# First attention of a vision tower on one core: whole-tile transfers of the operand parts, gathered by the reads, and projections by three products of split operands

## What is computed

```python
h = _L0_tok_ref(x, ...)                      # token mixer (attention-free), layer norm
h = concatenate([cls_tok, h], axis=1)        # one class token in front: 257 tokens
h = h + _L0_attn_ref(_layernorm(h), Wq, Wkv, Wout)
h = h + _L0_ffn_ref(_layernorm(h), ...)      # latent attention, then 8 experts, top 2

def _L0_attn_ref(tokens, Wq, Wkv, Wout):     # the "first attention"
    q = split_heads(tokens @ Wq, HEADS)      # 16 heads of 16
    kv = split_heads(tokens @ Wkv, HEADS)
    k, v = (kv[..., :DK], kv[..., DK:])      # 16 and 64 wide
    q, k, v = (l2norm(q), l2norm(k), l2norm(v))
    sim = jnp.einsum('bhid,bhjd->bhij', q, k)
    attn = jnp.square(jax.nn.relu(sim))
    out = tanh_norm(jnp.einsum('bhij,bhjd->bhid', attn, v))
    return merge_heads(out) @ Wout
```

## Time and profile before

| | |
|---|---|
| median of three runs | 3128.6 us (3127.97 to 3133.56) |
| the profiled execution | 3139.85 us, of which the profiled span is 3138.1 us |
| constants | 0 to about 52 us of the span |
| mixer and first attention, 32 samples | about 52 to 1630 us |
| PE busy over the span | 2907.1 us, 93% |
| DVE, ACT, POOL busy | 67%, 46%, 37% |

### The profile page before, as it was taken

One profiled execution on the slowest core, in us unless ns is written; L12 is line 12 of the kernel. 1 busy time (PEld: TensorE's weight loads), 2 busy tenths in 40 slices (PEclk: granted clock), 3 DMA queues, 4 the chain that ended last, 5 costly groups with the idle time before them and its releaser, 6 DMA issues. The chain is left out here.

```text
span 3138.1 us, 66657 instructions
## 1 busy us (share of the span) xinstructions
PE 2907.1 (93%) x21548; PEld 2217.3 (71%) x21549; DVE 2098.8 (67%) x5372; ACT 1442.7 (46%) x2948; POOL 1157.0 (37%) x966
## 2 busy tenths in 40 slices
PE   3899999999999999999966999999999972999998
PEld 1677777777777777777744666666766652999997
DVE  4577677677677777777734777777777855444444
ACT  0444544545545545445422555555555533444443
POOL 3324434434434334334321233333233324444443
PEclk7899999999999999999987999999999985999999
DMA  3424424424424424324302111111111101554544
GB/s 83 96 70 92 107 66 95 107 62 98 102 62 104 98 66 104 94 70 104 87 22 51 49 47 53 43 42 52 45 54 47 44 33 44 77 76 76 77 77 69
DMA packets 161126, 223.12 MB, mean 71 GB/s; under 512 B 30305, under 2 KB 125730, under 8 KB 161074
## 3 DMA queue, kind: packets, MB, share of 16 engines
q1 hardware_dynamic: 135138, 187.50, 23.9%
q0 software_dynamic: 25936, 34.95, 7.2%
HBM read 125.26 MB, written 97.08 MB: 71 GB/s over the span
## 5 line engine op out<-in xcount | busy, mean ns | idle before, releaser
L66 POOL TENSOR_TENSOR vrn<-vsm,inv_root 128x16 f32<-128x16 f32 x64 | 243.8, 3809 | 285.8 <-DVE vsm L836 285.8
L665 ACT ACTIVATE R<-psA 128x1024 f32<-128x1024 f32 x256 | 262.4, 1025 | 168.4 <-PE psA L1150 164.2
L857 DVE TENSOR_TENSOR PR<-R 128x1024 f32<-128x1024 f32 x256 | 321.3, 1255 | 0.0
L2512 POOL DMA_INDIRECT out_rows<-e_y,e_dest x137 | 213.7, 1560 | 289.8 <-DMA out_rows<-e_y,e_dest 182.2
L1904 DVE TENSOR_REDUCE m_nm<-psC 128x4 f32<-128x1028 f32 (+1 forms) x256 | 239.0, 956 | 72.0 <-PE psC L2177 71.4
L1165 PE MATMUL psA<-PR,V 128*64 128x258 f32 x2048 | 283.4, 398 | 0.0
L670 ACT ACTIVATE oTs<-psA 128x258 f32<-128x258 f32 x256 | 99.1, 387 | 358.1 <-PE psA L1165 352.3
L1783 ACT ACTIVATE m_PT<-psC 128x770 f32<-128x770 f32 x256 | 194.0, 810 | 137.3 <-PE psC L2205 137.3
L1210 PE MATMUL psA<-wout,OT 128*128 128x256 f32 x1024 | 244.6, 382 | 0.4 <-DVE OT L899 0.4
L1698 POOL DMA_INDIRECT xg<-tn,idx x124 | 124.5, 1004 | 318.6 <-DMA xg<-tn,idx 186.6
L1210 PEld LDWEIGHTS psA<-wout,OT 128*128 128x128 f32 x1024 | 188.7, 191 | 24.6 <-DVE OT L899 0.7
(11 more groups left out here) (417 smaller groups left out, 7633.0 us busy)
## 6 DMA issues: line engine op xcount, KB each, us to landing
ks<-kparts SPq DMA_DIRECT2D x256, 128.0 KB, 3.3
qs<-qparts SPq DMA_DIRECT2D x256, 128.0 KB, 3.8
e_x<-xg SPq DMA_DIRECT2D x143, 129.0 KB
xraw<-in_x SPq DMA_DIRECT2D x66, 256.0 KB
qparts<-qh SPq DMA_DIRECT2D x128, 128.0 KB, 2.4
kparts<-kh SPq DMA_DIRECT2D x64, 128.0 KB, 2.5
kparts<-kl SPq DMA_DIRECT2D x64, 128.0 KB, 2.4
qparts<-ql SPq DMA_DIRECT2D x64, 128.0 KB, 2.4
```

Source lines behind the costliest of these rows:

```text
L66: return pool.tensor_tensor(out, x, e.to_broadcast(list(out.shape)), ALU.pow)
L665: act.activation(R[:, p % 2].rearrange("p a t n -> p t a n"), ps[:, 0:2, :].rearrange("p t (a n) -> p t a n", a=2), ACT.Relu).then_inc(rel ...
L857: dve.tensor_tensor(PR[:, p % 2, :, :, 0:L], R[:, p % 2], R[:, p % 2], ALU.mult).then_inc(prob_done, 1)
L2512: pool.indirect_dma_start(out, bass.IndirectOffsetOnAxis(ap=dest[:, b % XD:b % XD + 1], axis=0), y[:, b % XD], None, compute_op=ALU.add).t ...
```

## The change

Five edits are made.

1. Each part goes to DRAM in one transfer of 128 partitions with 2 KB each (`keep_part`), so five stores instead of ten. `kh` is stored at `k_sq` and `qh` (twice) at `q_sq`, not after the lows. The DRAM tensors `kparts` and `qparts` have the head half `hh` as their first index, then the part n, so that one part lies in DRAM in two blocks of 64 rows.
2. The loads collect, for each of 32 partitions, four pieces of 1 KB instead of one of 4 KB (`heads`).
3. `project` uses split weights `wqkh`, `wqkl` and split tokens `xh`, `xl`, three fp32r products for each fp32 one. It waits for `xl_done` where it waited for `xT_done`; `token_lows` is moved ahead of `result` and `keep_sums` on DVE.
4. The constants stage splits `wqk`: DVE makes `wqk_hi` and `wqk_lo` ahead of the sums of squares, ACT lays both out by head (8 more small copies at its end).
5. `psq` shares the memory of `prl`; `class_products` waits for `xT_done` itself.

```diff
-            def keep_parts(tiles, rows, out):
-                for n, part in enumerate(tiles):
-                    for hh in range(2):
-                        sp.dma_start(rows[:, hh, n].rearrange("c x n -> x c n"),
-                                     part[64 * hh:64 * hh + 64].bitcast(F32)).then_inc(out, 16)
+            def keep_part(part, rows, n, out):
+                sp.dma_start(rows[:, n], part[:].bitcast(F32).rearrange("p c n -> p (c n)")).then_inc(out, 16)
+
+            def heads(rows, hh, n, c):
+                return rows[hh, n:n + 2].rearrange("a (r m) (c n) -> c (a r) m n", m=4, c=KT)[c]
...
-                        sp.dma_start(ks[to:to + 32, 4 * c:4 * c + 4].bitcast(F32).rearrange("p m n -> p (m n)"),
-                                     v.kparts[c, hh].rearrange("a (r m) n -> (a r) (m n)", m=4)).then_inc(moved, 16)
+                        sp.dma_start(ks[to:to + 32, 4 * c:4 * c + 4].bitcast(F32),
+                                     heads(v.kparts, hh, 0, c)).then_inc(moved, 16)
...
                 if c == 0:
+                    sp.wait_ge(k_sq, j + 1)
+                    keep_part(kh, v.kparts, 0, k_out)
                     sp.wait_ge(kl_done, j + 1)
-                    keep_parts((kh, kl), v.kparts, k_out)
+                    keep_part(kl, v.kparts, 1, k_out)
+                    sp.wait_ge(q_sq, j + 1)
+                    keep_part(qh, v.qparts, 0, q_out)
+                    keep_part(qh, v.qparts, 2, q_out)
                     sp.wait_ge(ql_done, j + 1)
-                    keep_parts((qh, ql, qh), v.qparts, q_out)
-                    sp.wait_ge(k_out, 64 * j + 64)
+                    keep_part(ql, v.qparts, 1, q_out)
+                    sp.wait_ge(k_out, 32 * j + 32)
                     lay_out_keys(0, moved0)
-                    sp.wait_ge(q_out, 96 * j + 96)
+                    sp.wait_ge(q_out, 48 * j + 48)
                     lay_out_queries(0, moved0)
...
                 prob(i, d, 5)
+                if more:
+                    token_lows(j)
                 if before:
                     result(i - 1)
                 keep_sums(i, d, 0)
                 if more:
-                    token_lows(j)
                     key_lows(j)
                     query_lows(j)
...
             def project(bank, first, done):
                 for c in range(2):
+                    sums = ps[:, bank, c * L:(c + 1) * L]
+                    cols = slice(first + c * P, first + (c + 1) * P)
                     for k in range(KT):
-                        last = pe.matmul(ps[:, bank, c * L:(c + 1) * L], v.wqk[:, k, first + c * P:first + (c + 1) * P],
-                                         xT[:, k, :], start=k == 0, stop=k == KT - 1)
+                        pe.matmul(sums, v.wqkh[:, k, cols], xh[:, k, :], start=k == 0, stop=False)
+                        pe.matmul(sums, v.wqkl[:, k, cols], xh[:, k, :], start=False, stop=False)
+                        last = pe.matmul(sums, v.wqkh[:, k, cols], xl[:, k, :], start=False, stop=k == KT - 1)
                 last.then_inc(done, 1)

             def project_keys(j):
-                pe.wait_ge(xT_done, j + 1)
+                pe.wait_ge(xl_done, j + 1)
                 project(BKT, 256, kT_done)
...
+            dve.tensor_copy(wqk_hi[:], wqk0[:]).then_inc(wqk_high, 1)
+            dve.wait_ge(wqk_high, 1)
+            dve.tensor_tensor(wqk_lo[:], wqk0[:], wqk_hi[:].bitcast(F32), ALU.subtract).then_inc(wqk_high, 1)

             dve.wait_ge(cls_sq, 2)
...
-    v.kparts = nc.dram_tensor("kparts", (KT, 2, 2, P // 2, L), F32, kind="Internal").ap()
-    v.qparts = nc.dram_tensor("qparts", (KT, 2, 3, P // 2, L), F32, kind="Internal").ap()
+    v.kparts = nc.dram_tensor("kparts", (2, 2, P // 2, KT * L), F32, kind="Internal").ap()
+    v.qparts = nc.dram_tensor("qparts", (2, 3, P // 2, KT * L), F32, kind="Internal").ap()
```

More of the change, by code:

```diff
@@ L71, in load_constants @@
         wqk0 = sbuf(nc, ctx, "wqk0", [P, KT, 512])
+        wqk_hi = sbuf(nc, ctx, "wqk_hi", [P, KT, 512], F32R)
+        wqk_lo = sbuf(nc, ctx, "wqk_lo", [P, KT, 512])
         v.wv = sbuf(nc, ctx, "wv", [P, KT, 1024])
@@ L102, in load_constants @@
          cls_stats, cls_norm, cls_T, cls_Tc, cls_proj, cls_sq, cls_ss, cls_rn, cls_unit, cls_vb, cls_mul, cls_sum,
-         cls_pair, cls_step, cls_v, identr, cls_lift, cls_rstd, powers, wv_high, ew_done) = sems(
+         cls_pair, cls_step, cls_v, identr, cls_lift, cls_rstd, powers, wv_high, ew_done, wqk_high) = sems(
             nc, ctx, "zeroed", "tables", "ld_bd", "ld_w", "ld_mask", "ld_bias", "ld_cls", "all_rows",
@@ L106, in load_constants, with by_half, by_head @@
             "cls_sq", "cls_ss", "cls_rn", "cls_unit", "cls_vb", "cls_mul", "cls_sum", "cls_pair", "cls_step", "cls_v",
-            "identr", "cls_lift", "cls_rstd", "powers", "wv_high", "ew_done")
+            "identr", "cls_lift", "cls_rstd", "powers", "wv_high", "ew_done", "wqk_high")
+        def by_half(w):
+            return w.rearrange("p (a h r e g) -> p h e a g r", a=4, h=2, e=2, g=2)
+        def by_head(w):
+            return w.rearrange("p (a g h e r) -> p h e a g r", a=4, g=2, h=2, e=2)
         block = ctx.enter_context(nc.Block())
@@ L214, in _ @@
                     for e in range(2):
-                        act.activation(v.wqk[:, k].rearrange("p (a h r e g) -> p h e a g r", a=4, h=2, e=2, g=2)[:, h, e],
-                                       wqk0[:, k].rearrange("p (a g h e r) -> p h e a g r", a=4, h=2, e=2, g=2)[:, h, e],
+                        act.activation(by_half(v.wqkh[:, k])[:, h, e], by_head(wqk0[:, k])[:, h, e],
                                        ACT.Copy)
@@ L225, in _ @@
                 act.activation(v.ewT[:, s, :], ps[:, s, 0:L], ACT.Exp).then_inc(ew_done, 1)
+            act.wait_ge(wqk_high, 2)
+            for k in range(KT):
+                for h in range(2):
+                    for e in range(2):
+                        act.activation(by_half(v.wqkl[:, k])[:, h, e], by_head(wqk_lo[:, k])[:, h, e], ACT.Copy)
         @block.vector
@@ L401, in mixer_and_attention @@
         prl = sbuf(nc, ctx, "prl", [CROWS, L])
-        psq = sbuf(nc, ctx, "psq", [CROWS, L])
+        psq = prl
         racl = sbuf(nc, ctx, "racl", [P, LT, HEADS])
@@ L501, in lay_out_queries @@
                         to = 64 * hh + at
-                        sp.dma_start(qs[to:to + 32, hh, 4 * c:4 * c + 4].bitcast(F32).rearrange("p m n -> p (m n)"),
-                                     v.qparts[c, hh, n:n + 2].rearrange("a (r m) n -> (a r) (m n)",
-                                                                        m=4)).then_inc(moved, 16)
+                        sp.dma_start(qs[to:to + 32, hh, 4 * c:4 * c + 4].bitcast(F32),
+                                     heads(v.qparts, hh, n, c)).then_inc(moved, 16)
             def spread_heads(j, c):
                 if c == 0:
+                    sp.wait_ge(k_sq, j + 1)
+                    keep_part(kh, v.kparts, 0, k_out)
                     sp.wait_ge(kl_done, j + 1)
-                    keep_parts((kh, kl), v.kparts, k_out)
+                    keep_part(kl, v.kparts, 1, k_out)
+                    sp.wait_ge(q_sq, j + 1)
+                    keep_part(qh, v.qparts, 0, q_out)
+                    keep_part(qh, v.qparts, 2, q_out)
                     sp.wait_ge(ql_done, j + 1)
-                    keep_parts((qh, ql, qh), v.qparts, q_out)
-                    sp.wait_ge(k_out, 64 * j + 64)
+                    keep_part(ql, v.qparts, 1, q_out)
+                    sp.wait_ge(k_out, 32 * j + 32)
                     lay_out_keys(0, moved0)
-                    sp.wait_ge(q_out, 96 * j + 96)
+                    sp.wait_ge(q_out, 48 * j + 48)
                     lay_out_queries(0, moved0)
@@ L1094, in project_values @@
                 if n == 0:
-                    pe.wait_ge(xh_done, j + 1)
                     need(pe, h2_done, j - 1)
@@ L1106, in project_values @@
                     pe.matmul(ps[:, bank, :], xh[:, k, t * P:(t + 1) * P], v.wvl[:, k, cols], start=False, stop=False)
-                if n == 0:
-                    pe.wait_ge(xl_done, j + 1)
                 for k in range(KT):
@@ L1127, in class_products @@
                 pe.wait_ge(k_lift, j + 1)
+                pe.wait_ge(xT_done, j + 1)
                 for k in range(KT):
@@ L2664, in first_weights @@
 def first_weights(nc, ctx, v):
-    v.wqk = sbuf(nc, ctx, "wqk", [P, KT, 512])
+    v.wqkh = sbuf(nc, ctx, "wqkh", [P, KT, 512], F32R)
+    v.wqkl = sbuf(nc, ctx, "wqkl", [P, KT, 512], F32R)
     v.wvh = sbuf(nc, ctx, "wvh", [P, KT, 1024], F32R)
```

## The result

The changed kernel takes **3789.9 us** in the median (3788.0 to 3797.5) against 3128.3 for the kernel before: the ratio is 1.212 [1.209, 1.214], 662 us more. The profiled execution took 3788.5 us around a span of 3787.0. (In a later series two executions of the kernel before, of 4446 and 7077 us, lie far off all others and stand in no comparison.)

What follows compares the result with a forecast made beforehand. PE set the pace, with the keys' and queries' round trip through DRAM right behind it. Stores on two engines would add 664 (31 periods) + 19.4 (first sample) + 1.5 (constants) = 685 us to 3128.6: 3814 us, range 3660 to 3940.

Steps and rivals of the forecast that it cites:

- The stores on two engines: Part stores in the attention stage: outermost dimension 2 gives each two DMA engines, 5.6 us of packets; chance 0.84.
- The line of five: Five stores queue on the same two engines: 5 x 5.6 + 1.4 = 29.4 us from squared keys until `q_out` is full.
- the 1.4 us fixed: Part of a store's landing that is not packets, split off from the 2.1 us of the `hs` store.
- The loads unchanged: Gathering loads of four 1 KB pieces still land in 3.8 us; bound above +2.4 us per sample.
- The period: One sample's time on PE rises from 47.26 to 67.2 us, plus up to 1.5 us for half clock.
- The round trip: From squared keys through DRAM to `sim(j, 0)`: 34.5 us against 14.3 before.
- PE's own part: PE's work from `sim(j, 0)` to the next squared keys: 32.7 us, plus up to 1.5 for half clock.
- the restart after the wait of 3.55 us: In the first sample, PE's clock stood at 0.50 for 3.0 us after waiting; taken to cost up to 1.5 us per period.
- The sum: Whole kernel: 664 us for 31 periods + 19.4 first sample + 1.5 constants = 685 us more, giving 3814 us.
- The projections: Keys' and queries' projections: 24 fp32r products take 2.74 instead of 3.35 us; net gain 0.5 us while PE sets the pace.
- The stores run on 16 engines after all: Rival for the part stores: each takes 2.1 us, PE keeps the pace, 20 us off, 3109 us; chance 0.10.
- moves nothing that can be told: Rival: 16 engines, but the gather lands 0.5 us after PE is ready in each sample, 3123 to 3134 us; chance 0.02.

Runs made afterwards that it cites:

- The ladder: Kernel before plus eight single 256 KB transfers at its end, DRAM side in 2 to 32 blocks or 128 rows: stores from 2 blocks 7.9 us, from 32 blocks 2.4.
- the stores in halves: Changed kernel with each part stored in two transfers of 64 rows instead of one of 128: 3135.9 us, 1.000 of the kernel before.
- blocks of four: Changed kernel with four whole stores to 32 DRAM blocks of four rows, second query pair read by two loads of 16 rows: 3134.2 us, 1.000 of the kernel before.
- the narrow products apart: Whole stores to 32 DRAM blocks of four rows, plus the class token's eight 16-column products moved ahead of its two wide ones: 3109.4 us, 0.993 of the kernel before.
- the products alone: Kernel before with only the three products of split operands, stores and loads as before: 3131.9 us (3114.3 to 3154.6), 1.001 of the kernel before.

## Why the prediction was right

**The stores on two engines: right.** The prediction inferred an engine count that follows the outermost dimension from the small packets of two transfers, and gave it 0.84. The ladder shows it step by step. The line of five was put at 29.4 us from the squared keys until `q_out` is full; SP goes on to the loads of queries 28.6 us after them (1174.63, the end of `ksq` on ACT, to 1203.21). Each store costs 5.3 to 5.45 us in the line instead of 5.6. Alone, with its landing, the ladder has 7.9 instead of 7.0: the 1.4 us fixed, split off from one store of `hs`, were too few, which the line of five hardly shows.

**The loads unchanged: right.** 4.9 us from their first issue to the next `sim(j, 0)` (1203.21 to 1208.08), predicted 1.3 + 3.8. The issues take 0.6 us instead of 0.43 each, and the landing 3.2 instead of 3.8; the two errors cancel.

**The period: right, with two small errors that cancel for the most part.** The round trip is 33.6 us (1106.29 to 1139.90; predicted 34.5). PE's own part is 34.7 us (1139.90 to 1174.63; predicted 34.2 with the clock). The clock stayed at half for 5.1 us instead of 3.0, which costs 1 us more, and the rest of PE's part was 0.5 us shorter. The earlier trace rows were read as the restart after the wait of 3.55 us; in fact the clock of that trace had fallen before the wait began, at about 97.4 us, in the norm products of 8 columns (0.82 from 97.00 to 97.60, and 0.50 from then on). Ahead of it stand the narrow products again, there with a wait of 0.65 us between the two groups, in the very trace from which the forecast was made. The sum is 68.3 us in this period and 68.2 in the mean of 31, predicted 68.7.

**The sum was 23 us too high.** 31 periods are longer by 20.7 us each by the first projections of the two traces, not 21.4: 0.5 by the period, and 0.2 because I set it against one period of 47.26 while the mean before is 47.47. The round trip that is left over, which I put on the first sample with 19.4 us, costs 16.5 behind the last sample's first projection. Up to the first sample's first projection 1.8 us are lost (82.90 against 81.13; 1.5 predicted for the constants): 1.2 before PE's first product, the rest by the wait for `xl`, less what an earlier rise of the clock gave back. 641 + 16.5 + 1.8 = 659 us up to the latent attention. The medians differ by 662, the two profiled spans only by 649: the profiled run before was 11 us above its median, and its later stages took 11 us longer than those of the changed kernel's.

**The projections: the mechanism was right.** 24 products in 2.82 us (2.74 predicted), and PE waits for `xl` in two samples of 32 only, 3.1 us in all. The undisturbed period of the kernels with short stores says that they give 0.7 us per sample, not 0.5.

**What the prediction missed lies in a rival.** *The stores run on 16 engines after all* was put at 3109 us. Run as such, with the stores in halves or in blocks of four, it came out at 3136 and 3134. With the blocks of four its waits and its PE work were as described; the granted clock took the gain back, which neither this rival nor the forecast had in it. With the narrow products apart it is 3109.4. So with quick stores this rival's time would have been some 25 us too low, and the case "moves nothing that can be told" (3123 to 3134 us) would have come nearest, for a reason that it didn't name.

## What to carry to other kernels

Before merging transfers, look at the outermost dimension of each side, as the access pattern has it, and not at the bytes (here only the DRAM side was varied): one transfer of 256 KB with two outermost blocks took 7.9 us, the same bytes in 32 blocks 2.4. Count the small packets behind a transfer: they say how many engines it had. And when a kernel on which PE never idles gets less work but not less time, look at the granted clock window by window, and at the narrow products ahead of each fall; setting wide ones between them cost nothing here.

## What was not expected of the hardware

**The issue itself blocks.** With two stores outstanding on the same two engines, SP's next issue takes 3.2 to 5.5 us instead of 0.50 to 0.56: the five stores above have 0.56, 0.50, 8.49 for two, and 5.45. The first load of keys behind them takes up to 5.0 us as well, where the others take 0.6. The kernel should lose nothing by it, because SP would wait for `q_out` anyway (argued from SP's order, not tried), but whatever else stands in SP's order would.

**The clock falls while PE is busy.** The Trainium skill ("TensorE: Matmul & The Clock Gate", "Part 1: The HAM clock gate (the "warmup" mystery)") explains half clock by idle time of the PE; in the rows above PE has work ahead of the fall and through it, with many narrow products, and no wait. Here the measurement decides, with one reserve: the profile models where a product ends, so its busy time doesn't tell how much of it the array worked. The fall goes with this order of products on three kernels; what about them brings it was not taken apart. It costs 1.2 us per fall, and if each sample had one it would be an estimated 38 us of this kernel (32 x 1.2): the slowest run of the products alone, 3154.6 us, has a mean clock of 0.947, the quickest, 3114.3, one of 0.963. What stays open is why the row of falls sets in at another sample in each run (near 560, 1030 and 1180 us in the three profiled ones, each of another kernel); that it starts when drift brings the narrow group to the right place is argued from the periods, not shown.
